# Two neighbouring pairs of steps change places in the order of TensorE and one pair in that of ScalarE, in the first attention stage of a two-layer gated block

## The reference

```python
x = x + tanh(g_xattn[0]) * _L0_xattn_ref(_layernorm(x), ctx, ctx, ...)
x = x + tanh(g_ffn[0])   * _L0_ffn_ref(_layernorm(x), ...)      # routed experts + shared expert
x = x + tanh(g_xattn[1]) * _L1_xattn_ref(_layernorm(x), ctx, ctx, mask, ...)
x = x + tanh(g_ffn[1])   * _L1_ffn_ref(_layernorm(x), ...)      # fake-quantised

def _L0_xattn_ref(q, k, v, ...):
    wq, wk, wv = heads(q @ wq_w.T + wq_b), heads(k @ wk_w.T + wk_b), heads(v @ wv_w.T + wv_b)
    probs = softmax(einsum('bthd,bshd->bhts', wq, wk) / sqrt(DH))
    return einsum('bhts,bshd->bthd', probs, wv).reshape(b, t, d) @ wo_w.T + wo_b

# routing of the first feed-forward part
scores = sigmoid(x @ gate_weight.T)      # 64 experts, 8 groups, 4 groups kept, 8 experts kept
```

## Time and profile before

| | |
|---|---|
| median of three runs | 1928.83 us |
| the profiled execution's own time | 1926.39 us |
| its span, first to last instruction | 1924.6 us |
| PE busy | 1731.2 us, 90% |
| DVE busy | 1383.7 us, 72% |
| ACT busy | 1178.2 us, 61% |
| POOL busy | 611.8 us, 32% |
| mean granted TensorE clock | 0.975 of full |

### The profile page before, as it was taken

How to read it: one execution, slowest core, us unless ns; L and a number is a source line. 1 busy time by engine, 2 the same in 40 slices (tenths; PEclk the granted TensorE clock), 3 DMA queues, 4 the chain that set the end, 5 groups by cost and what they waited for, 6 DMA issues and landing times.

```text
span 1924.6 us, 54303 instructions
## 1 busy us (share of the span) xinstructions
PE 1731.2 (90%) x20208; PEld 1336.6 (69%) x20208; DVE 1383.7 (72%) x4587; ACT 1178.2 (61%) x2411; POOL 611.8 (32%) x616
## 2 busy tenths in 40 slices
PE   5999999999998299999999997599999999978855
PEld 4777777777777288888888886377777777743334
DVE  4888888888888456644444443488888888859988
ACT  3777777777776133332323222488888888858875
POOL 1000000000000146666666665322222222211147
PEclk9999999999999699999999999699999999989989
DMA  3222333222234568888778774332232323203265
GB/s 100 74 91 94 97 94 105 91 91 91 94 96 136 158 176 211 210 208 203 199 201 200 199 198 98 105 92 91 86 97 84 98 85 94 73 26 164 99 246 192
DMA packets 231349, 247.63 MB, mean 129 GB/s; under 512 B 29681, under 2 KB 207217, under 8 KB 228913
## 3 DMA queue, kind: packets, MB, share of 16 engines
q1 hardware_dynamic: 206272, 205.54, 33.1%
q0 software_dynamic: 24816, 38.62, 10.8%
HBM read 142.40 MB, written 101.66 MB: 127 GB/s over the span
## 4 chain that ended last, share of the span: by engine, by line
PE 47%; DVE 33%; ACT 7%; issue 6%; POOL 4%; SPq 1%; DMA 1%; POOLq 0%; DVEq 0%; ACTq 0%
DVE mt L800 15%; PE tiles L384 8%; PE bank L449 6%; ACT pt L582 6%; PE bank L1310 5%; PE tiles L1285 4%; PE tiles L367 4%; PE bank L1253 3%; PE tiles L351 3%; PE bank L479 3%; PE bank L1320 3%; DVE hmax L1731 3%; POOL rstd L1991 2%; PE bank L1297 2%; DVE h_ring L1724 2%
## 5 line engine op out<-in xcount | busy, mean ns | idle before, releaser
L1991 POOL TENSOR_TENSOR rstd<-var,minus_half 128x2 f32<-128x2 f32 x139 | 97.2, 699 | 736.5 <-DVE var L879 723.3
L800 DVE TENSOR_REDUCE mt<-tiles 128x16 f32<-128x2048 f32 x128 | 293.4, 2293 | 30.5 <-PE tiles L367 30.0
L582 ACT ACTIVATE pt<-tiles 128x2048 f32<-128x2048 f32 x128 | 240.7, 1881 | 49.1 <-PE tiles L384 49.1
L1516 POOL DMA_INDIRECT accumulator<-ye,tid x128 | 208.6, 1629 | 152.0 <-DVE ye L1449 132.2
L1449 DVE TENSOR_SCALAR ye<-bank,xr 128x256 f32<-128x256 f32 x128 | 56.0, 479 | 247.3 <-PE bank L1297 116.9
L384 PE MATMUL tiles<-qm,qkp 32*128 32x128 f32 x4096 | 151.1, 284 | 18.8 <-DVE mt L800 18.7
L384 PEld LDWEIGHTS tiles<-qm,qkp 32*128 32x128 f32 x4096 | 126.6, 187 | 48.3 <-DVE mt L800 33.7
L1501 POOL DMA_INDIRECT xr<-token_rows,tid x128 | 137.3, 1073 | 70.3 <-issue 38.5
L449 PE MATMUL bank<-xt,w_q 128*128 128x128 f32 x1024 | 154.8, 285 | 0.9 <-ACT xt L590 0.9
L367 PE MATMUL tiles<-qkp 32*128 32x256 f32 x2048 | 151.1, 408 | 3.3 <-ACT qkp L604 3.3
L449 PEld LDWEIGHTS bank<-xt,w_q 128*128 128x128 f32 x1024 | 131.8, 195 | 14.9 <-issue 13.3
(11 more groups left out here) (247 smaller groups left out, 4078.2 us busy)
## 6 DMA issues: line engine op xcount, KB each, us to landing
keys_values<-res SPq DMA_DIRECT2D x64, 256.0 KB
cxax<-accumulator SPq DMA_DIRECT2D x128, 128.0 KB, 2.2
cxax<-keys_values SPq DMA_DIRECT2D x128, 128.0 KB, 2.5
hidden_away<-h_ring SPq DMA_DIRECT2D x8, 1536.0 KB, 5.1
token_rows<-pay SPq DMA_DIRECT2D x64, 160.0 KB, 1.8
pt<-in_expert_up SPq DMA_DIRECT2D x36, 256.0 KB
cxax<-in_ctx SPq DMA_DIRECT2D x64, 128.0 KB, 2.2
res<-in_x SPq DMA_DIRECT2D x64, 128.0 KB, 2.3
```

The costliest lines, as they stand in the source:

```text
L582: nc.scalar.activation(pt[r % 2][:, :, :], tiles[:, :, :], ACT.Exp).then_inc(sem("exp_done"), 1)
L800: nc.vector.tensor_reduce(mt[:, :].rearrange("p (i n c) -> p i n c", i=RT, n=2 * KC)[:, :, :, 0], tiles[:, :, :].rearrange("p i (n k) -> p ...
L1516: nc.gpsimd.indirect_dma_start(out=acc[p][:, :], out_offset=bass.IndirectOffsetOnAxis(ap=tid[b % 8][:, h:h + 1], axis=0), in_=ye[r][:, h, ...
L1991: G.tensor_tensor(rstd[:, :], var[:, :], minus_half[:, :], ALU.pow).then_inc(sem(f"rstd_step_{L}"), 1)
```

## The change

On TensorE, `heads_to_tokens(o)` and `project_v(f)` change places, and `moe_logits(v)` and `transposes(f)` change places. On ScalarE, `router_tanh(v)` and `copy_xt(f)` change places. No instruction is added or removed, and no wait is changed. VectorE, GpSimd and SyncE keep their order.

```diff
@@ attention_pe, body, L == 0
                     moe_counts(u)
+                    heads_to_tokens(o)
                     project_v(f)
-                    heads_to_tokens(o)
+                    transposes(f)
                     moe_logits(v)
-                    transposes(f)
                     scores_t(k)
@@ attention_act, body, L == 0
                     copy_v(f)
                     normalise_second(w)
+                    copy_xt(f)
                     router_tanh(v)
-                    copy_xt(f)
                     copy_at(o)
```

## The result

| | before | changed |
|---|---|---|
| median | 1929.86 us (4 runs) | 1951.02 us (4 runs, 1948.71 to 1952.06) |
| ratio | | 1.011, 95% interval 1.0092 to 1.0128 |
| span of the profiled execution | 1924.6 us | 1947.1 us |
| slot of the stage, L800 to L800 in the steady part | 9.35 us | 9.70 us |
| PE busy, of the span | 90% | 89% |

The account below looks back on a forecast made before the run. VectorE and TensorE both bound the 9.35 us slot; TensorE's stretch grows from 2.26 to 2.86 us, less 0.19 us of slack: 0.41 us x 59 = 24.2 us on 1926.39 us; against the median 1953, predicted 1952, range 1941 to 1962.

Parts of the forecast that it names:

- Step 1: TensorE, heads to tokens L490 now ahead of L460: 0.49 us to the next step, no wait.
- Step 2: TensorE, projection L460 to transposes L429 with copy L630 between: 1.69 - 0.10 for loaded weights = 1.59 us.
- Step 3: TensorE, transposes L429 to logits L523: 0.42 us less 0.13 of overlap, 0.29 us.
- Step 4: TensorE, logits L523 to transposed scores L384: 0.49 us.
- The cover: TensorE's slack in the 9.35 us slot, its own loop being 9.16 us: 0.19 us a slot.
- The number of slots: First attention stage, slots with both transposes and logits, from the sixth: 64 - 5 = 59, at 0.41 us each.
- the release: Delay until TensorE goes on after another engine finishes what it waits for: about 0.15 us.
- The reserve at L500: Head normalisation L910 was to be in time for TensorE's L500 by only 0.07 us.
- the dearer case: Rival: L910, behind L922's wait for the tanh, comes too late for L500; 35 us more, 1963 us; 13%.
- The cheaper rival: Rival: L429's stall costs less because more weights load meanwhile; +0.25 us a slot, 15 us, 1943 us; 14%.

Follow-up runs that it names:

- without the wait: Changed order with the values projection writing bank 5 instead of bank 4, counts moved behind the logits: 1925.72 us, ratio to before 0.9970.
- the kernel with less in the loop: Projection into bank 5, then logits, heads to tokens, transposes, counts; router's transposes ahead of L384; ScalarE's copies follow: 1912.46 us, ratio to before 0.9917.
- the copy twice in the order of before: The kernel before plus one scratch copy of the projected values on ScalarE ahead of L630: 1930.21 us, ratio to before 1.0007.
- the first four kernels: Follow-ups: first exchange only 1928.21 us, second only 1929.52, changed order with projection in bank 5 1925.72, changed with head normalisation ahead of routing 1949.06.

## Why the prediction was right

**The direction and the mechanism** held. L429 waits for L630, L384 no longer waits for the maxima, and without the wait the changed order costs nothing (9.35 us).

**Step 1**, L490: 304.50 to 304.99, 0.49 us as taken, no wait.

**Step 2**, L460 to L429: 1.59 us as taken from the first slot of before, with the 0.10 for loaded weights (L460 took 1.03 us). The wait that comes of it is 0.55 us in each of 56 slots (0.6 forecast), and ScalarE's wait at L630 is 0.57 (0.5 forecast).

**Step 3**, L429 to L523: 0.24 us, I took 0.29. This is 0.05 of the 0.06 us between the slot of 9.76 us that I forecast and the 9.70 measured. The 0.13 us of overlap that I took there lay between two rows and was a guess; it was 0.17, as at L523 to L429 in the flow.

**Step 4**, L523 to L384: 0.49 us as taken.

**The cover.** Taken as 0.19 us from one slot near the end of the stage; the kernel with less in the loop has 9.15 us in its steady slots, which makes it 0.21. The three kernels whose delay stayed under it (either exchange alone, the copy twice in the order of before; each 0.16 to 0.19 us) lost nothing, and the wait of L384 for the maxima, 16.4 us in the steady stretch before, is down to 0.6, 0.6 and 1.2 us in them. That is the cover being used up.

**The number of slots** was 59. 59 x 0.35 = 20.6 us; by the traces these slots took 18.7 us more. The first three of them lost 0.5 us together in place of 1.0, one in the middle nothing, and near the end one with a transfer in its way took less than before (10.72 us after, 11.45 before). So the forecast of 24.2 us was 5.5 too much for the stage: 3.6 from the 0.06 us a slot, 1.9 from these slots.

**The time.** The interval of the ratio is 18 to 25 us, which holds 18.7, 20.6 and 24.2 alike, so it is the slots and not the medians that tell them apart. That 1951.02 us is only 1 us from the forecast of 1952 is luck in part: the increase was 3 us smaller than forecast, and the kernel before, which the forecast put at 1928, measured 1929.86 beside the changed one. The other stages and the start, which the prediction put at nothing, came out 1.7 and 2.2 us longer in the profiled executions.

**VectorE.** I put L922 about 0.7 us later and its new wait at about 0.4; the wait was 0.60. The 0.4 is worked out nowhere, and the prediction's own times give 0.64: L922 at 307.13, behind L901, which ended at 306.24 + 0.25 = 306.49 in the trace of before. As forecast it didn't set the slot, and the maxima were in time by 0.35 us with the release counted, as forecast. The reserve at L500 was larger than the 0.07 us that I gave it: L910 ended at 307.81 + 0.42 = 308.23, 0.18 us ahead of L500 at 308.41. I had charged 0.15 us for the release, which is ScalarE's; VectorE's to TensorE took 0.05 in the earlier trace rows (maxima ended at 306.33, L384 at 306.38), which leaves 0.13. So the dearer case had more room than the prediction gave it.

**Weights during the wait.** The trace of the changed kernel decides like that of before: in the wait the weight load of L429 started at 306.55, behind the copy, and not during it. The cheaper rival had nothing from it.

**Which part costs.** Neither exchange alone costs anything (9.35 us each). The two together take away both fillers between the projection and the transposes, 0.44 and 0.39 us of TensorE's time, as the trace of before has them (L523 starts at 305.33 and L429 at 305.72):

```profile
304.89 0.60 PE L490 MATMUL bank<-ident,ovs 128*128 128x128 f32 x4
```

With one filler left the stretch up to L384 grows by 0.19 us at most, with none by 0.55 (304.50 to 307.31 is 2.81, before 2.26). The delays don't add up, they overlap with the round trip, and only together do the exchanges exceed the cover. The prediction priced the pair and was silent on this.

## What to carry to other kernels

Work that stands between a producer and the step that waits for its round trip over another engine is not idle filler: count it against the length of that round trip (here 1.59 us) before moving it, and then against the cover of the engine (here 0.2 us). What exceeded both was paid in every slot here, one for one. And before taking a small step off a chain, look whether the step behind it would start any earlier: a start that is set by the latency of its own operand gained only 0.02 us here.

## What the runs showed that I had not expected

The first slots of the stage vary between executions by several us: the maxima of the sixth slot started between 56.8 and 65.2 us in the profiled executions, with the granted clock between 25 and 40 us at 0.61 to 1.00 of full. The two go together: the three executions at 0.61 to 0.63 started late (62.1 to 65.2), the two at 0.77 at 59.8 and 60.1, the five at 0.89 and above at 58.2 or earlier. TensorE was idle for a large part of the time before (busy about 9 us of the 15 from 10 to 25 us), but so it was in all ten, and which of them then fell to the lower level for longer isn't explained by it. The times of whole runs show the same: of the 27 runs of before beside the first four kernels, the three with a mean granted clock of 0.975 took 1925.5 to 1926.0 us, the 22 with 0.973 or less 1927.8 to 1934.6. Differences of 3 us between kernels are better read from the length of a steady slot, which repeats within about 0.01 us.

VectorE's instruction that reads what the one before it wrote, and waits for its semaphore, started 0.51 us behind the start of that one (a residual over 128x256 of 0.48 us). With a small independent step in between, which itself started 0.40 us behind, it was 0.54. So the step of 0.21 us cost 0.03 us.
